# Diffusion-transformer block pair: where the transposes, the first exponentials and the weight loads of the first layer stand in their queues

## The reference

```python
def _attn(xq, ctx, wq, wkv, wo, bo):
    q = _heads(xq @ wq)
    k, v = jnp.split(ctx @ wkv, 2, axis=-1)
    k = _heads(k)
    v = _heads(v)
    q = _rope(q, sq, cq)
    k = _rope(k, sk, ck)
    sim = jnp.einsum('bhnd,bhmd->bhnm', q, k) * DH ** (-0.5)
    a = jax.nn.softmax(sim, axis=-1)
    o = jnp.einsum('bhnm,bhmd->bhnd', a, v)
    o = o.transpose(0, 2, 1, 3).reshape(xq.shape[0], xq.shape[1], MID)
    return o @ wo + bo
...
attn_in = _adaln(x, cond, ln1_w, ln1_b, g1_w, g1_b, b1_w, b1_b)
x = _attn(attn_in, attn_in, sa_wq, sa_wkv, sa_wo, sa_bo) + x
cross_in = _adaln(x, cond, ln1_w, ln1_b, g1_w, g1_b, b1_w, b1_b)
ctx_n = _ln(context, ca_lnc_w, ca_lnc_b)
x = _attn(cross_in, ctx_n, ca_wq, ca_wkv, ca_wo, ca_bo) + x
```

## Time and profile before

| | |
|---|---|
| median of 3 runs | 402.15 us |
| the profiled execution's own time | 401.46 us |
| its span | 399.5 us |
| PE busy | 379.3 us, 95% of the span |
| DVE busy | 319.9 us, 80% |
| ACT busy | 296.3 us, 74% |
| POOL busy | 149.2 us, 37% |
| granted clock of PE, mean | 0.996 |

### The profile page before, as it was taken

One profiled execution on the slowest core, in us unless ns is written; L12 is line 12 of the kernel. 1 busy time (PEld: TensorE's weight loads), 2 busy tenths in 40 slices (PEclk: granted clock), 3 DMA queues, 4 the chain that ended last, 5 costly groups with the idle time before them and its releaser, 6 DMA issues.

```text
span 399.5 us, 9926 instructions
## 1 busy us (share of the span) xinstructions
PE 379.3 (95%) x3597; PEld 285.7 (72%) x3597; DVE 319.9 (80%) x702; ACT 296.3 (74%) x1031; POOL 149.2 (37%) x132
## 2 busy tenths in 40 slices
PE   7989999999999999999999998988999999999987
PEld 3557777767777877777777757775778777788665
DVE  4998998988998898989898958764657888888741
ACT  2377787786887777878877794779779787987932
POOL 4363523323634323635244425341266550302120
PEclk9989999999999999999999999999999999999999
DMA  7133333332334233232221211000000000000001
GB/s 232 51 114 114 120 109 126 104 108 102 110 108 133 80 120 110 103 106 87 86 74 62 74 43 38 2 2 1 2 2 2 2 2 2 2 2 3 2 0 53
DMA packets 17474, 25.89 MB, mean 65 GB/s; under 512 B 3632, under 2 KB 6195, under 8 KB 17427
## 3 DMA queue, kind: packets, MB, share of 16 engines
q1 hardware_dynamic: 17106, 25.05, 18.6%
q10 hardware_dynamic: 288, 0.22, 0.3%
q0 software_dynamic: 32, 0.00, 0.0%
HBM read 8.48 MB, written 0.52 MB: 23 GB/s over the span
## 4 chain that ended last, share of the span: by engine, by line
PE 52%; DVE 20%; ACT 16%; issue 8%; POOL 2%; DVEq 0%; POOLq 0%
PE bank L966 41%; ACT prob L443 7%; PE bank L1052 6%; DVE qk L755 4%; PE bank L1260 4%; DVE prob L733 3%; DVE nmax L843 3%; ACT raw L535 2%; DVE qk L746 2%; DVE xn L669 2%; POOL xn L286 1%; PE bank L977 1%; DVE x L649 1%; DVE st L654 1%; ACT L414 1%
## 5 line engine op out<-in xcount | busy, mean ns | idle before, releaser
L305 POOL TENSOR_TENSOR swp<-swp,small 128x512 f32<-128x512 f32 x62 | 78.6, 1279 | 129.6 <-PE bank L966 98.6
L443 ACT ACTIVATE prob<-bank,nmax 128x128 f32<-128x128 f32 x256 | 91.2, 390 | 1.2 <-DVE nmax L726 1.2
L535 ACT ACTIVATE raw<-bank,nmax 128x128 f32<-128x128 f32 x256 | 72.7, 389 | 11.7 <-DVE nmax L843 11.4
L443 ACT ACTIVATION_READ_ACCUMULATOR prob<-bank,nmax 128x1 f32 x256 | 59.2, 231 | 0.0
L843 DVE TENSOR_REDUCE nmax<-bank 128x4 f32<-128x512 f32 x64 | 41.1, 684 | 17.1 <-PE bank L966 17.1
L726 DVE TENSOR_REDUCE nmax<-bank 128x4 f32<-128x512 f32 x64 | 41.2, 685 | 16.7 <-PE bank L966 16.6
L733 DVE TENSOR_TENSOR prob<-prob,rz 128x512 f32<-128x512 f32 x64 | 48.7, 761 | 2.2
L966 PE MATMUL bank<-hT,wqkv 128*128 128x512 f32 x96 | 50.0, 605 | 0.3 <-DVE qk L746 0.3
L449 ACT ACTIVATE probT<-bank 128x512 f32<-128x512 f32 x32 | 19.1, 597 | 37.9 <-PE bank L1052 37.9
L1052 PEld LDWEIGHTS bank<-small,prob 128*128 128x128 f32 x256 | 28.6, 140 | 24.5 <-DVE prob L733 14.4
L279 POOL TENSOR_TENSOR rstd<-vare,neg_half 128x4 f32<-128x4 f32 x12 | 12.3, 1029 | 90.1 <-DVE vare L661 90.0
(11 more groups left out here) (112 smaller groups left out, 636.2 us busy)
## 6 DMA issues: line engine op xcount, KB each, us to landing
swp<-raw SPq DMA_DIRECT2D x124, 128.0 KB, 2.1
wqkv<-in_wqkv SPq DMA_DIRECT2D x16, 256.0 KB, 2.9
wff<-in_wff SPq DMA_DIRECT2D x4, 256.0 KB, 3.0
x<-in_x SPq DMA_DIRECT2D x2, 256.0 KB, 4.1
wmod<-in_wmod SPq DMA_DIRECT2D x2, 256.0 KB, 2.7
ctx<-in_ctx SPq DMA_DIRECT2D x1, 384.0 KB, 5.6
ctxT<-in_ctxT SPq DMA_DIRECT2D x1, 384.0 KB, 3.4
wsq<-in_wsq SPq DMA_DIRECT2D x1, 320.0 KB, 3.2
```

The lines of the kernel that those rows point to most:

```text
L305: nc.gpsimd.tensor_tensor(four(swp[:, m % 2, f, :]), four(swp[:, m % 2, f, :]), sin[f], ALU.mult).then_inc(rope_sin[f], 1)
L443: last = nc.scalar.activation(prob[:, hh, bcols(u)], S[hh][:, bcols(u)], ACT.Exp, bias=nmax[:, s % 2, hh, u:u + 1], accum_out=zsum[:, s % ...
L535: last = nc.scalar.activation(prob1[:, s % 2, hh, bcols(u)], score_bank(s, hh)[:, bcols(u)], ACT.Exp, bias=nmax[:, s % 2, hh, u:u + 1])
```

## The change

Three edits, all in the first layer. The transposes of head 0 of item s leave PE's slot s, where they stood behind the fills, and stand in slot s + 1 behind the scores, ahead of the transposes of head 1. On ACT the exponentials of head 0 go ahead of the copy of T[1], and wait now for the transposes of head 0 of the item before, since they write the buffer that these read. On SP the load in slot m waits until the swaps of that slot have landed, where it waited for the scores of item m - 1 (the first load waited for POOL's sine).

```diff
@@ SP
-            sp.wait_ge(rope_sin[1], 1)
+            sp.wait_ge(swapped[1][1], 32)
             loads(0)
             for m in range(2, ITEMS):
                 swap(m)
                 if m <= 23:
-                    sp.wait_ge(scores[0], m)
+                    sp.wait_ge(swapped[1][m % 2], 32 * swaps(m))
                     loads(m - 1)
...
@@ ACT, l0_slot
                 if s >= 2:
                     evacuate_o(s - 2)
                 if s >= 1:
+                    act.wait_ge(probs_T[0], s)
+                exp0(s, 0)
+                if s >= 1:
                     copy_T0(s - 1)
-                exp0(s, 0)
...
@@ PE, l0_slot
                 if s >= 1:
+                    transpose_probs(s - 1, 0)
                     transpose_probs(s - 1, 1)
...
-                if s == 31:
-                    prob_values(s - 1)
-                transpose_probs(s, 0)
-                if 1 <= s < 30:
+                if 1 <= s <= 31 and s != 30:
                     prob_values(s - 1)
...
@@ PE, l1_slot
                 if s == 0:
+                    transpose_probs(ITEMS - 1, 0)
                     transpose_probs(ITEMS - 1, 1)
```

## The result

The changed kernel takes 406.58 us (median of 4 runs, 406.18 to 407.16) against 402.00 for the kernel before in the same session: ratio 1.0109, 95% interval 1.0092 to 1.0126. It is slower, as forecast, but by twice as much: +4.6 us where +2.3 was predicted, 0.6 us above the range. The profiled execution took 406.21 us with a span of 404.4, 4.9 us more than before.

The account below looks back on a forecast made before the run. PE was taken to bound the kernel (52% of the wait chain, alone setting the pace in eight clean slots). Terms 2.3 + 0 - 0.4 - 0.1 + 0.9 + 0 - 0.3 = +2.4, taken as +2.3 us: median 404.45, range 401.0 to 406.0.

Parts of the forecast that it names:

- the mechanism: First layer: the value fill waits for ACT's copy of T[1], now behind the exponentials, by 0.13 to 0.18 us.
- the clean slots: Eight first-layer slots where PE alone sets the pace: 6.65 to 6.93 us each, +2.3 us together (+0.7 to +2.8).
- the move of the transposes: PE, head 0's transposes moved behind the next scores: by itself worth 0 per slot, bounds -0.09 and +0.06 us.
- the fill may start at 3.96 us: Clean slots: value fill starts 3.96 us into the slot, after ACT's copy, where PE would arrive at 3.78 to 3.83.
- costs nothing: ACT's new wait for head 0's transposes is over by about 1.79 us, before the exponentials can start at 1.91.
- The weight loads' 0.10 us: PE's uncovered weight loads at the value fill and the products: 0.10 us each; slot 6.74 us if neither is paid.
- The five slots with waits: Slots 7, 12, 19, 20, 27, where a transpose waits for DVE's normalise: 34.65 against 34.7 us, 0 (down to -1.0).
- The five slots that end on ACT: Slots 4, 6, 8, 13, 21, whose products wait for ACT's evacuation: together -0.4 us.
- Slot 29 and the end: Slot 29: value fill delayed behind ACT's exponentials and copy, +0.9 us; slots 30 and 31: 0 (-0.3 to +0.5).
- The start: Slots 0 and 1: 0.5 us of PE work leaves the path, the copy holds the fill 0.4: -0.3 us (±1.0).
- another stretch of low clock: Sign of being wrong: slot 1's stretch at granted clock 0.50, seen at 25.9 to 27.6 us, differs after the change.
- The clock rival: Slot 1: PE's lower clock begins sooner or lasts 2 us longer, 1 us more, median 405.4; chance with late end 0.12.

Follow-up runs that it names:

- edit 1 alone: Kernel before with only head 0's transposes moved behind the next slot's scores, ACT's copy of T[1] still ahead of the exponentials: 406.31 us, ratio 1.0096.
- edit 2 alone: Kernel before with only head 0's exponentials put ahead of ACT's copy of T[1], PE's order unchanged: 412.95 us, ratio 1.0275.
- edit 2 undone from slot 29 on: Changed kernel with the copy of T[1] back ahead of head 0's exponentials from slot 29 on only: 405.79 us, ratio 1.0115.
- the keys first: Changed kernel with PE filling keys ahead of values: 401.93 us, ratio 1.0004. As a variant of the kernel before, the same swap there: 402.50 us, ratio 1.0015.
- edits 1 and 2 together: Changed kernel with the loads' waits as before, so only the moved transposes and the reordered exponentials: 406.60 us, ratio 1.0131.
- the loads alone: Kernel before with only the loads made to wait for the landing of their slot's swap: 402.54 us, ratio 1.001.
- the keys first and the copy in the middle: Changed kernel with keys filled ahead of values, the copy of T[1] amid head 0's exponentials, and loads as before: 403.41 us, ratio 1.0057.
- the copy in the middle: Changed kernel with ACT's copy of T[1] between the second and third of head 0's four exponentials: 402.28 us, ratio 1.0015.
- the copy one instruction later: Changed kernel with ACT's copy of T[1] one instruction later, behind the raw queries: 414.80 us, ratio 1.0338.

## Why the prediction was right and wrong

**The sign and the mechanism were right.** The value fill waits for the copy, released by ACT's line, in the clean slots; slots 8, 18 and 20 no longer wait for the normalise; the second layer takes the same time; slot 29's value fill is 5.04 us behind its scores where it was 4.02. One term of the sum was wrong without harm: the move of the transposes, priced at 0, costs nearly 4 us in edit 1 alone. With edit 2 the exponentials no longer stand behind them, and that loss is gone.

**The clean slots were under-priced: 3.3 us, not 2.3.** The failed step is "the fill may start at 3.96 us": it starts at 4.11. Two of its terms were too short. The 0.72 us from maxima to exponentials measures 0.79 here, and the 0.06 from ACT's end to PE's start measures 0.14. Together they are the 0.15.

Neither is scatter; both came from instructions with fewer waits. The 0.72 stands in slot 0, where the first exponential waits for one semaphore, and the trace of before has 0.71 to 0.73 at 25 places of the second layer, all with one. Edit 2 gives it a second wait. In each of slots 1 to 28 of the changed kernel the distance is 0.78 to 0.80, and the same with edit 2 alone, where the transposes that it waits for are done a slot earlier; slot 0, without that wait, keeps 0.73. So the sentence that the new wait "costs nothing" was wrong by 0.07 us a slot. The 0.06 is from a projection with one wait, the value fill has three. The first line below is ACT's end ahead of that projection, the others are a wait for ACT in slot 6 of the kernel before, at products with three waits:

```profile
234.56 0.58 ACT L453 ACTIVATE oT<-bank 128x512 f32<-128x512 f32 x1
...
65.58 0.81 ACT L483 ACTIVATE ctxnT<-bank,small 96x512 f32<-96x512 f32 x1
...
66.53 1.09 PE L966 MATMUL bank<-probT,v 128*64 128x128 f32 x16 [0.31 <-ACT ctxnT L483]
```

The first ends at 235.14, 0.05 us ahead of PE; the second at 66.39, 0.14 ahead. Of the matmuls of the kernel before that wait for ACT, the six with one wait start 0.05 to 0.06 us behind ACT's end, the seven with two to five 0.14 to 0.26. So the right prices were in the trace of before. That the number of waits sets them is read from these comparisons; no run isolates it, and some instructions with two or three waits, released by other engines, start after 0.04 to 0.06 us all the same.

The whole effect is the difference between a gate near 4 and PE's arrival near 3.8, so an error of 0.15 is nearly that effect again. The upper bound of 2.8 us (7.00 a slot) stretched neither term. The weight loads' 0.10 us, which I had counted as doubtful, were right (0.97 and 0.96 us).

**The five slots with waits: +0.57, not 0.** All five take 7.06 after, where before they took 7.12, 6.79, 6.93, 7.06 and 6.83. That they come to the length of the clean slots shows that the gate sets them too. At 6.93 they would have come to 0, as forecast; this is the same error, five times 0.13.

**The five slots that end on ACT: +0.4, not -0.4.** Slot 21 shows the common part: the exponentials start 0.5 us earlier in it than before, yet the products wait for ACT and start at 6.80 instead of 6.82 us. The copy has only moved behind the exponentials, and ACT's chain is as long.

```profile
174.86 0.37 ACT L443 ACTIVATE prob<-bank,nmax 128x128 f32<-128x128 f32 x1 [1.26 <-DVE nmax L728]
...
178.57 0.87 ACT L425 ACTIVATE hT<-bank,mod 128x128 f32<-128x128 f32 x2
...
179.69 1.09 PE L968 MATMUL bank<-probT,v 128*64 128x128 f32 x16 [0.68 <-ACT hT L425]
```

I had expected 0.11 us a slot from that chain; the 0.07 us of the second wait took most of it. Slot 4 alone lost 0.40: DVE, late from the collision in slot 3, starts its maxima at 1.56 us instead of 1.19.

```profile
46.92 1.28 DVE L728 TENSOR_REDUCE nmax<-bank 128x4 f32<-128x512 f32 x2
```

Slot 6 lost 0.20, with the maxima at 1.33 instead of 1.19. These two losses belong to this execution: in the run with edit 2 undone from slot 29 on, the same code up to there, the maxima of both start at 1.19, slots 4 and 6 take 7.83 and 7.66, and the five together 38.80, which is -0.1 against before. So of the +0.4, read against that trace, 0.5 is where the swaps landed and -0.1 the change. The prediction had no term for DVE and POOL meeting, though it moved the normalise and the trace of before shows such meetings. The Trainium skill (SBUF — State Buffer, section "SBUF: two separate sides") says that a DVE instruction with two inputs in SBUF and a GpSimd instruction that reads SBUF take a shared pair of ports as an exclusive lock, for the whole instruction. The traces agree: in both slots above the second comer takes 0.54 us longer, near the normalise's 0.69, and the sums run in full (1.16 us) only behind the sine.

**Slot 29 and the end: +1.07 and +0.21 against +0.9 and 0.** Slot 29 is off by the same short distances. Slot 31's 0.2 us is not the gate, for it appears also with the keys first (7.39). It comes with edit 1: every kernel with it takes 7.31 to 7.55 there (7.50 with edit 1 alone), every kernel without it 7.16 to 7.20.

**In all.** The forecast missed 2.5 us of the span. The gate is some 1.8 of that (1.0 in the clean slots, 0.6 in the five with waits, 0.2 in slot 29), the five slots that end on ACT 0.8, slots 9 and 31 0.3; the start gave 0.3 back.

**The start: -0.59, inside its bounds, by luck.** One sign of being wrong was badly chosen: I wrote that I would be wrong if slot 1 had another stretch of low clock. It had one only in place. Windows of slot 1 after (busy of PE, PEld, DVE, ACT, POOL, granted clock, DMA share, GB/s), beside the earlier trace rows:

```profile
23.70:25.90 2.20, 2.19 (x21) 1.98 (x22) 2.13 (x10) 0.00 (x0) 0.88 (x1) 0.71 0.53 195
25.90:27.60 1.70, 1.70 (x7) 1.11 (x5) 1.70 (x4) 1.53 (x9) 1.70 (x2) 0.50 0.24 53
27.60:31.00 3.40, 3.40 (x28) 2.04 (x26) 3.30 (x13) 3.04 (x12) 1.07 (x2) 0.94 0.26 94
```

In windows of a tenth of a microsecond the 0.50 lies from 24.6 to 28.0 us after, and from 25.8 to 29.2 before: 1.2 us earlier, 3.4 us long both times.

But the stretch belongs to the execution and not to the change. Of the four timed executions of the changed kernel only the profiled one has a mean granted clock under 1.00, and so have 8 of the 29 of the kernel before in one session. The traces of edits 1 and 2 together and of edit 2 undone from slot 29 on have no such stretch, with the same idle time of 1.85 us ahead of the scores. There slot 1 takes 7.42 us, with the stretch 7.44: without it PE only waits longer for ACT's copy, here with edits 1 and 2.

```profile
28.18 1.13 PE L968 MATMUL bank<-wqkv,hT 128*128 128x128 f32 x8 [1.26 <-ACT probT L449]
```

The kernel before has no such wait to hide it: slot 1 takes 8.02 us with the stretch, and 6.99 and 7.06 in the two one-edit variants of it (the loads alone, the keys first) whose traces have none. From these, at full clock the changed kernel would start some 0.4 us later than the kernel before, not 0.6 sooner; the 0.5 us that should have left the path is lost at the gate. The whole doesn't follow the stretch: those 8 executions have a median span of 399.45 us, the other 21 one of 399.6. The clock rival did not happen. Nor did eight transposes in a row lower the clock: the page shows 9 from the fourth slice on.

**What stays open.** Why the second swap of some slots lands 3.0 to 3.9 us behind its issue (slot 3 after, slots 3 and 24 with the keys first, slot 24 with edit 1 alone), where the median is 2.1, and why these are other slots in another execution. And why the keys first and the copy in the middle lose together what neither loses alone.

## What to carry to other kernels

When an order change puts a wait near the point at which the waiting engine arrives anyway, the outcome is the difference of two nearly equal sums: read every distance between engines from a place where the waiting instruction has as many waits as it will have, and let the range carry its error times the number of repeats. A step moved on one engine moves what another engine reads from it: edit 1, free on PE, cost nearly 4 us, most of it through ACT. And if a late write stands in the way of a fill of the same bank, look first for other work to put in between: here one swapped line recovered all of it.

## What the hardware showed that I had not expected

- The distance from the start of the maxima's reduction to the first exponential is 0.72 us in slot 0 and 0.79 in slots 2 and 3, on the same two kinds of instruction with ACT idle in both; the first has one wait, the others two. From the end of ACT's copy to PE's first matmul behind it: 0.14 us with three waits, where 0.05 was seen with one.
- A gate passes its delay on in full: 0.48 us more on ACT gave 0.48 to 0.49 us more in each clean slot.
- DVE's normalise beside POOL's sine: started 0.01 us apart, the sine takes 1.81 instead of 1.27 us and the two rope sums behind 2.37 instead of 1.28; a normalise that meets a sine takes 1.74 instead of 0.69.
- A stretch of 3.4 us at a granted clock of 0.50 stands in slot 1 of four of the fourteen traces, in one of them (the copy one instruction later) ahead of slot 0, at 10.8 to 14.2 us, and in nine nowhere. Traces with the same code and the same idle time ahead have it or don't.
- One and the same piece of code has its late swaps, and with them the meetings of DVE and POOL, in other slots in another execution: with the sine as the second comer in slots 3 and 9 of one, 11 and 15 of the other. A slot that is 0.4 us longer in one trace need not be the change's.
